# Landmark attention layer: value blocks stationary in four column tiles, both attention maps divided by their sums before the difference

## The reference, cut to what matters

```python
xn = _rms(x, w_norm_in)                      # x * rsqrt(mean(x*x) + 1.19e-07) * w
ssm_out = <running mean over the tokens, a decay for each head>
q1, q2, k1, k2 = xn @ slr_wq1, xn @ slr_wq2, xn @ slr_wk1, xn @ slr_wk2   # 32 features each
v = xn @ slr_wv                                                             # 32 features
a1 = softmax(q1 @ k1.T * sc);  a2 = softmax(q2 @ k2.T * sc)                 # 512 x 512 each
slr_out = ((a1 - slr_lam * a2) @ v) @ slr_wo
mixed = ssm_out + (p_medium + p_full) * slr_out     # p: a small router; plus a landmark term on the last token
out = concatenate([mixed, xn]) @ mix_w
out = residual + _rms(out, w_norm_out)
out = out + 0.1 * <the mean of out over the tokens, through three 128 x 128 matrices>
```

## Time and profile before

| what | us |
|---|---|
| median of 3 runs (2606.91 to 2615.31) | 2607.51 |
| the profiled execution, its own time | 2612.94 |
| its span in the trace | 2611.2 |
| the layer in question, 1269.7 to 1418.2 of the span | 148.5 |
| PE busy in the layer | 136.8 |
| DVE busy in the layer | 80.1 |
| ACT busy in the layer | 53.9 |
[...]

### The profile page before, as it was taken

How to read it: one execution, slowest core, us unless ns; L and a number is a source line. 1 busy time by engine, 2 the same in 40 slices (tenths; PEclk the granted TensorE clock), 3 DMA queues, 4 the chain that set the end, 5 groups by cost and what they waited for, 6 DMA issues and landing times. The chain is left out here.

```text
span 2611.2 us, 30132 instructions
## 1 busy us (share of the span) xinstructions
PE 2225.1 (85%) x9848; PEld 923.0 (35%) x9888; DVE 1703.9 (65%) x2464; ACT 1216.5 (47%) x2420; POOL 699.1 (27%) x658
## 2 busy tenths in 40 slices
PE   8999999947469989787998779988878988878877
PEld 2333224312122224354454234433324436533332
DVE  5666665568877745653463664569995446569995
ACT  4655663258557853221342225346655422246653
POOL 1111110042211110121100010049981013149882
PEclk9999999979889989897866889999999999999989
DMA  3000000033000010000000000022220000012220
GB/s 162 1 1 1 1 1 1 1 49 50 1 2 1 1 59 38 1 1 1 0 1 1 1 0 1 0 74 98 87 69 1 0 1 2 1 62 94 93 78 17
DMA packets 24281, 68.64 MB, mean 26 GB/s; under 512 B 2816, under 2 KB 9024, under 8 KB 23360
## 3 DMA queue, kind: packets, MB, share of 16 engines
q1 hardware_dynamic: 23264, 65.94, 8.2%
q10 hardware_dynamic: 864, 0.79, 0.3%
HBM read 58.78 MB, written 1.57 MB: 23 GB/s over the span
## 5 line engine op out<-in xcount | busy, mean ns | idle before, releaser
L3816 POOL TENSOR_TENSOR l_drive<-l_du,l_bsb 128x1024 f32<-128x1024 f32 x126 | 296.4, 2374 | 41.4 <-DVE l_du L3717 26.3
L3568 DVE TENSOR_TENSOR_SCAN l_state<-l_decay,l_drive 128x1024 f32<-128x1024 f32 x128 | 289.9, 2278 | 10.0 <-ACT l_decay L3509 9.3
L3398 PE MATMUL l_py<-l_state,w_const 128*128 128x512 f32 x512 | 256.9, 628 | 41.5 <-DVE l_state L3576 29.8
L241 POOL TENSOR_TENSOR l_nx_small<-l_nx_small,w_norm 128x4 f32<-128x4 f32 x50 | 53.4, 1068 | 866.4 <-DVE l_nx_small L234 866.4
L403 ACT ACTIVATE l_probs<-l_psp,l_stats 128x512 f32<-128x512 f32 x256 | 173.1, 683 | 147.1 <-DVE l_stats L413 147.1
L3509 ACT ACTIVATE l_decay<-l_delta,l_a 128x511 f32<-128x511 f32 x256 | 164.9, 680 | 119.8 <-DVE l_state L3568 119.6
L1324 DVE TENSOR_REDUCE l_tops<-l_ring 128x2 f32<-128x1024 f32 x128 | 151.5, 1220 | 45.6 <-PE l_ring L1315 45.2
L411 DVE TENSOR_REDUCE l_stats<-l_psp 128x2 f32<-128x1024 f32 x128 | 156.1, 1219 | 29.3 <-PE l_psp L363 28.9
L760 DVE SCALAR_TENSOR_TENSOR l_product<-l_psu,w_gated,l_first 128x512 f32<-128x512 f32 x104 | 78.0, 750 | 131.8 <-ACT l_first L734 131.5
L1396 ACT ACTIVATE l_shared<-l_ring 128x512 f32<-128x512 f32 x256 | 139.0, 598 | 46.1 <-PE l_ring L1386 45.9
L3398 PEld LDWEIGHTS l_py<-l_state,w_const 128*128 128x128 f32 x512 | 100.3, 200 | 153.8 <-issue 87.1
(11 more groups left out here) (623 smaller groups left out, 4242.5 us busy)
## 6 DMA issues: line engine op xcount, KB each, us to landing
l_bsb<-l_rows SPq DMA_DIRECT2D x64, 512.0 KB, 3.7
l_csb<-l_rows SPq DMA_DIRECT2D x32, 256.0 KB, 3.1
l_stack<-l_parts SPq DMA_DIRECT2D x84, 64.0 KB
w_gated<-in_gated SPq DMA_DIRECT2D x1, 3297.5 KB, 10.3
w_mha<-in_mha SPq DMA_DIRECT2D x1, 2568.5 KB, 11.4
w_ssm<-in_ssm SPq DMA_DIRECT2D x2, 1171.0 KB, 14.3
w_moe<-in_moe SPq DMA_DIRECT2D x1, 2248.0 KB, 18.3
w_const<-in_const SPq DMA_DIRECT2D x1, 1131.0 KB, 13.6
```

Of the source, the lines that this page charges most:

```text
L3398: mm = pe.matmul(py[:, t, :], eye, state[:, k % STATES, t, :], start=False, stop=k % NS == NS - 1, skip_group_check=True)
L3568: dve.tensor_tensor_scan(state[:, k % STATES, :, :].rearrange("p t s -> p (t s)"), decay[:, k % 2, :, :].rearrange("p t s -> p (t s)"), dr ...
L3816: pool.tensor_tensor(drive[:, k % RING, :, :], du[:, :, :], bsb[:, k // 2 % RING, k % 2, :].unsqueeze(1).to_broadcast([P, CT, S]), ALU.mult)\
```

## The change

`average` takes the value block (128 x 32) as the stationary operand and the whole turned map row block (512 columns) as the moving one: four matmuls, each into its own 32 PSUM partitions, one for each key block, in column tiles 0, 32, 64 and 96 of the array. The sum over the key blocks is left to `project_ctx`, whose weight `wo` is now stacked four times (K = 128). With the features already on partitions, `turn_ctx` and `divide_ctx` go, and the batch's chain has one step less; STEPS is 25. `differ` divides each map by its own sum before subtracting, with one more DVE instruction over 128 x 512. `var_in` and `var_out` take the form of `NextNorm.var`: the constant stationary in four column tiles, 128 columns moving, and DVE picks each row's own token with two instructions in place of one. `make_diag_out`, `nx.keep` and `nx.diag` go from DVE to ACT (`keep_by_scalar` L208, `diag_by_scalar` L251: four instructions with 128 x 128 elements each).

New steps: average 4b+6 with take_ctx in the same step, project_ctx and join_parts 4b+7, join and take_mix 4b+8, var_out, eps_out and rstd_out 4b+9, spread_out and make_diag_out 4b+10, bus and scale_out 4b+11, take_bus and finish 4b+12, centre, square and keep 4b+13, nx.var 4b+14, nx.eps, nx.rstd and nx.diag 4b+15, nx.spread and nx.scale 4b+16. On ACT a step is: exp_scores, take_bus, take_turn, take_ctx, take_mix, make_diag_out, nx.square and keep, nx.diag.

```diff
@@ var_in (var_out likewise, on sq_out and mx)
-                mm = pe.matmul(bank(b)[:, t:t + 1], sq[:, b, tok(t)], mean, start=True, stop=True, skip_group_check=True)
+                mm = pe.matmul(bank(b)[t * QUAD:(t + 1) * QUAD, 0:P], mean, sq[:, b, tok(t)], start=True, stop=True,
+                               skip_group_check=True, tile_position=(0, t * QUAD))
@@ average
-            for t in range(TT):
-                for o in range(TT):
-                    mm = pe.matmul(mx[:, b % 2, t * SH:(t + 1) * SH], turned[:, b % 2, o, tok(t)], v[:, b, o, :],
-                                   start=o == 0, stop=o == TT - 1, skip_group_check=True)
+            for o in range(TT):
+                mm = pe.matmul(mx[o * SH:(o + 1) * SH, b % 2, :], v[:, b, o, :], turned[:, b % 2, o, :], start=True, stop=True,
+                               skip_group_check=True, tile_position=(0, o * SH))
             mm.then_inc(L["averaged"].sem, 1)
-        def turn_ctx(pe, b):
-            pe.wait_ge(L["ctx"].sem, L["ctx"].at(0, b + 1))
-            for t in range(TT):
-                mm = pe.transpose(mx[0:SH, b % 2, tok(t)], ctx[:, t, :], eye)
-            mm.then_inc(L["ctx_turn"].sem, 1)
@@ spread_out
-            pe.wait_ge(L["diag_out"].sem, L["diag_out"].at(0, b + 1))
+            pe.wait_ge(L["diag_out"].sem, L["diag_out"].at(0, TT * (b + 1)))
@@ take_ctx
-            act.wait_ge(L["ctx_turn"].sem, L["ctx_turn"].at(0, b + 1))
+            act.wait_ge(L["averaged"].sem, L["averaged"].at(0, b + 1))
             act.wait_ge(L["slr"].sem, L["slr"].at(0, b))
-            act.activation(ctx_t[:, :], mx[0:SH, b % 2, :], ACT.Copy).then_inc(L["ctx_sb"].sem, 1)
+            act.activation(ctx_t[:, :], mx[:, b % 2, :], ACT.Copy).then_inc(L["ctx_sb"].sem, 1)
@@ eps_in (eps_out likewise)
-            dve.tensor_scalar(small[:, b, 0, :], bank(b)[:, 0:TT], RMS_EPS, None, ALU.add).then_inc(L["eps"].sem, 1)
+            dve.scalar_tensor_tensor(own_in[:, b, :], bank(b)[:, 0:P], RMS_EPS, own, ALU.add, ALU.mult)\
+                .then_inc(L["own"].sem, 1)
+            dve.wait_ge(L["own"].sem, L["own"].at(0, b + 1))
+            dve.tensor_reduce(small[:, b, 0, :], own_in[:, b, :].rearrange("p (j c) -> p j c", j=TT), AX.X, ALU.add)\
+                .then_inc(L["eps"].sem, 1)
@@ differ
-            dve.reciprocal(ratio[:, 0:1], second).then_inc(L["ratio"].sem, 1)
-            dve.wait_ge(L["ratio"].sem, L["ratio"].at(0, 2 * u + 1))
-            dve.scalar_tensor_tensor(out=ratio[:, 1:2], in0=first, scalar=w("slr_lam"), in1=ratio[:, 0:1], op0=ALU.mult,
-                                     op1=ALU.mult).then_inc(L["ratio"].sem, 1)
-            dve.wait_ge(L["ratio"].sem, L["ratio"].at(0, 2 * u + 2))
-            dve.scalar_tensor_tensor(out=probs[:, u % 3, 0, :], in0=probs[:, u % 3, 1, :], scalar=ratio[:, 1:2],
-                                     in1=probs[:, u % 3, 0, :], op0=ALU.mult, op1=ALU.subtract)\
+            dve.reciprocal(ratio[:, :], sums[:, b % 2, :, t]).then_inc(L["ratio"].sem, 1)
+            dve.wait_ge(L["ratio"].sem, L["ratio"].at(0, 3 * u + 1))
+            dve.tensor_scalar(ratio[:, 1:2], ratio[:, 1:2], w("slr_lam"), None, ALU.mult).then_inc(L["ratio"].sem, 1)
+            dve.wait_ge(L["ratio"].sem, L["ratio"].at(0, 3 * u + 2))
+            dve.tensor_scalar(probs[:, u % 3, 1, :], probs[:, u % 3, 1, :], ratio[:, 1:2], None, ALU.mult)\
+                .then_inc(L["ratio"].sem, 1)
+            dve.wait_ge(L["ratio"].sem, L["ratio"].at(0, 3 * u + 3))
+            dve.scalar_tensor_tensor(out=probs[:, u % 3, 0, :], in0=probs[:, u % 3, 0, :], scalar=ratio[:, 0:1],
+                                     in1=probs[:, u % 3, 1, :], op0=ALU.mult, op1=ALU.subtract)\
                 .then_inc(L["mixp"].sem, 1)
-        def divide_ctx(dve, b):
...
@@ make_diag_out
+        def make_diag_out(act, b):
+            act.wait_ge(L["rstd_out"].sem, L["rstd_out"].at(0, b + 1))
+            act.wait_ge(L["spread_out"].sem, L["spread_out"].at(0, b))
+            to, mask = diag_out[:, :, :].rearrange("p t (j c) -> p t j c", j=TT), own_tokens(core)
+            for j in range(TT):
+                act.activation(to[:, :, j, :], mask[:, :, j, :], ACT.Copy, scale=small[:, B, 1, j:j + 1])\
+                    .then_inc(L["diag_out"].sem, 1)
@@ STEPS and the order of the steps
-        STEPS = TT * (inner - 1) + 18 if inner == B else TT * (B - 1) + 14
+        STEPS = TT * (inner - 1) + 17 if inner == B else TT * (B - 1) + 13
...
@@ weights
-                "wo": v[p + "slr_wo"], "r1": v[p + "router_w1"], "r2": v[p + "router_w2"],
+                "wo": np.tile(v[p + "slr_wo"], (TT, 1)), "r1": v[p + "router_w1"], "r2": v[p + "router_w2"],
```

More of the change, by code:

```diff
@@ L2202, in landmark_layer @@
     L = Layer(nc, name, core, ["slr"], **NextNorm.SIGNALS, **NextNorm.LAST, lam=2, chain=3, chain_sb=3,
-              sq=B, var=B, eps=B, rstd=B, diag=B, spread=B, xl=B, drive=B, ema=B, wide_q=B,
+              sq=B, var=B, own=B, eps=B, rstd=B, diag=B, spread=B, xl=B, drive=B, ema=B, wide_q=B,
               q=B, q_sb=B, k=B, k_sb=B, v_ps=B, v_sb=B,
               hid=1, hid_sb=2, lscore=1, arc=8, lexp=1, wide=3, logit=1, router=7, rexp=1,
-              scores=NU, highest=NU, top=NU, probs=2 * NU, ratio=2 * NU, mixp=NU, turn=NU, turn_sb=NU,
-              averaged=B, inv=B, ctx=B, ctx_turn=B, ctx_sb=B, slr=B, joined=2 * B, mix=B, sq_out=B, mix_sb=B,
-              var_out=B, eps_out=B, rstd_out=B, diag_out=B, spread_out=B, scaled=B, result=B, bus=B, bus_sb=B,
+              scores=NU, highest=NU, top=NU, probs=2 * NU, ratio=3 * NU, mixp=NU, turn=NU, turn_sb=NU,
+              averaged=B, ctx_sb=B, slr=B, joined=2 * B, mix=B, sq_out=B, mix_sb=B,
+              var_out=B, own_out=B, eps_out=B, rstd_out=B, diag_out=TT * B, spread_out=B, scaled=B, result=B, bus=B, bus_sb=B,
               done=B)
@@ L2240, in landmark_layer @@
         front = mx[:, 1, :]
-        nx = NextNorm(L, aux[:, :])
+        nx = NextNorm(L, aux[:, :], pieces=TT)
         late = NextNorm(L, aux[:, :], last=True, shared=nx)
         eye, ones = core.w("const", "eye"), core.w("norm", "ones")
-        mean = core.w("norm", "mean", 0, 1)
+        mean, own = core.w("norm", "mean"), core.w("norm", "own")
         score_scale = 1.0 / float(SH) ** 0.5
@@ L2665, in _ @@
                     if b is not None:
-                        turn_ctx(pe, b)
+                        project_ctx(pe, b)
                     b = batch_at(u, 8)
                     if b is not None:
-                        project_ctx(pe, b)
+                        join(pe, b)
                     b = batch_at(u, 9)
                     if b is not None:
-                        join(pe, b)
-                    b = batch_at(u, 10)
-                    if b is not None:
                         var_out(pe, b)
-                    b = batch_at(u, 14, inner)
+                    b = batch_at(u, 13, inner)
                     if b is not None:
                         nx.centre(pe, b)
-                    b = batch_at(u, 17, inner)
+                    b = batch_at(u, 16, inner)
                     if b is not None:
@@ L2683, in _ @@
                         turn(pe, u - 2)
+                    b = batch_at(u, 10)
+                    if b is not None:
+                        spread_out(pe, b)
                     b = batch_at(u, 11)
                     if b is not None:
-                        spread_out(pe, b)
-                    b = batch_at(u, 12)
-                    if b is not None:
                         bus(pe, b)
-                    b = batch_at(u, 15, inner)
+                    b = batch_at(u, 14, inner)
                     if b is not None:
@@ L2782, in _ @@
                     if b is not None:
-                        make_diag_out(dve, b)
-                    b = batch_at(u, 12)
-                    if b is not None:
                         scale_out(dve, b)
                     b = batch_at(u, 15, inner)
-                    if b is not None:
-                        nx.keep(dve, b)
-                    b = batch_at(u, 16, inner)
                     if b is not None:
@@ L2807, in _ @@
                     b = batch_at(u, 16, inner)
-                    if b is not None:
-                        nx.diag(dve, b)
-                    b = batch_at(u, 17, inner)
                     if b is not None:
@@ L2840, in _ @@
                 for u in range(STEPS):
-                    b = batch_at(u, 10)
+                    b = batch_at(u, 9)
                     if b is not None:
                         rstd_out(b)
-                    b = batch_at(u, 16, inner)
+                    b = batch_at(u, 15, inner)
                     if b is not None:
```

59 lines of the change are left out of this document (26 added, 33 removed).

## The result

The changed kernel takes 2589.3 us in the median of four runs (2586.2 to 2592.4), the kernel before 2608.9 on the same chip; the ratio is 0.9924, 95% interval 0.9907 to 0.9940. The forecast was 2596.2 with a range of 2585 to 2605. So the sign and the range held, but the gain is 19.6 us and not 11.3. The profiled execution spans 2587.0 us against 2611.2; that is 24.2, more than the medians' 19.6, mainly because the profiled execution of the kernel before was itself 4.0 us above its median (2612.94 against 2608.92).

A forecast was written before the change was run, and what follows sets the result against it. PE's queue was taken to set the layer's pace, at a mostly lower clock. Terms -1.5 + 0.7 - 4.7 - 0.5 - 1.9 - 3.4 summed to -11.3 us, from median 2607.51 to 2596.2, range 2585 to 2605.

The forecast's parts named there:

- Front: Layer's start: early variances shrink from 5.12 to under 2 us, some 2.3 reaching the first spread; -1.5 us, bounds -2.3 and 0.
- Steps 0 to 6: DVE's step grows from 2.44 to about 2.9 us, still under PE's 3.05; +0.7 us, bounds 0 and +1.3.
- First period: Average(0) to average(1): 23.5 us becomes 18.8 with the shorter average and no turn_ctx; -4.7 us.
- less 1.9 because the clock rose in its last part: Average(0) to average(1): 1.9 us taken off the lower-clock sums, 25.4 before and 20.2 after.
- Second period: Average(1) to average(2): less PE work, but a new 2.2 us wait at spread_out for ACT's diagonal; -0.5 us, bounds -2 and +2.
- Third period: Average(2) to average(3): work 18.9 to 16.2 us, waits 2.8 to 3.9; -1.9 us.
- Tail: Last average to layer end, at the lower clock: 31.7 us becomes 28.3, savings partly handed back by diagonals, epsilons and a wait; -3.4 us.
- The price of a switch between array shapes: PE's switch into and out of column tiles, read off another layer's row: at most 0.15 us.
- The likeliest case: The forecast itself: the layer's six parts sum to -11.3 us, giving 2596.2, own range 2592 to 2601; chance 0.53.
- the first rival: Narrow work kept the clock down; full-width tiles let it stay at 2.4 GHz through the batches: 2588 us, chance 0.20.
- The slower side: PE has more gaps and never gets the upper clock; layer's mean clock near 0.5: 2617 us, chance 0.07.
- The two remaining rivals: Half lost to PE waits as DVE's step passes PE's: 2602.5, chance 0.17; average's tiles not side by side: 2608, chance 0.03.

The follow-up runs named there:

- the repetition: The changed kernel run once more, word for word; layer 131.0 us instead of 126.5, ratio to the kernel before 0.9927 (0.9910 to 0.9943).

## Why the prediction was right or wrong, by its own steps

1. Front: -1.5 forecast with bounds of -2.3 and 0, -3.0 in the profile and -4.2 in the repetition. The work was priced right: four variances are 2.3 us of PE instead of 6.2, and the first spread comes 2.3 us earlier on the layer's own count, as forecast. But the clock did not rise "at the same moment as now": it rose 13.1 us into the layer before and 9.4 after, so the gain was not partly spent at a clock of 0.50.
2. Steps 0 to 6: +0.7 forecast, +1.0 measured, +1.6 in the repetition. The price of 0.48 us for the multiply was 0.486, and DVE's step is 2.96 us for 2.9, still under PE's 3.05.
3. First period: -4.7 forecast, -10.2 and -7.4 in two executions. This and the tail (6) are the terms that were mis-sized: together they gave 9.0 us more than forecast in the profile, of 11.4 in all, and 7.2 more in the repetition, of 6.9 in all. The step that failed here is "less 1.9 because the clock rose in its last part", kept the same before and after. The rise came 74.5 us into the layer before (1344.4 less 1269.9), 53.7 after (1325.9 less 1272.2) and 58.6 in the repetition, so 16 to 21 us earlier. The work that I took out was priced right: 2.0 forecast, 1.94 measured.
4. Second period: -0.5 forecast, -1.0 and +3.6. The new wait was foreseen with its cause and its place. In the repetition, with the average ahead of it at a clock of 0.50, it was 2.3 us against the 2.2 of the forecast; in the profile, with the average at 1.00, it is 2.8, because ACT was still busy with the exponentials for 0.5 us when the turn was done. POOL's power was done before. In all PE sat idle 4.2 us here, not 2.2; that the term came near the forecast in the profile is luck, since PE's work at a clock of 1.00 instead of 0.81 paid for it.
5. Third period: -1.9 forecast, -2.6 and -3.9. This agreement is luck too. PE's idle time was 7.9 us where 3.9 was forecast (2.6 instead of 1.0 ahead of the join, and 1.8 ahead of var_out that was not in the sum), and its work took 11.5 us where 16.2 was forecast, at a clock of 0.91 instead of 0.69. The term doesn't follow from its own numbers either: (16.2 + 3.9) less (18.9 + 2.8) is -1.6.
6. Tail: -3.4 forecast, -6.9 and -7.9. Again the clock. The step that failed is "At the lower clock after the last average starts": it was at 0.72 and 0.78, and the average itself took 1.07 us and not 2.1. Diagonals and waits came as priced or longer, with 1.9 and 2.3 us of PE idle ahead of the last two spread_out. "Is partly handed back by two diagonals" held in direction: with both diagonals on DVE the tail is 2.4 us shorter at the same clock of 0.72.

The step "that keep and diag leave DVE is worth nothing by itself here" held in that no gain came of it. By the ratios, the variances and the moves to ACT together changed nothing that can be measured (0.9924 with them, 0.9920 without).

The price of a switch between array shapes was read off a row whose neighbours are not whole-array work but bf16 matmuls with 64 rows, so it did not show what it was used for. The traces show it elsewhere: ahead of a tiled group a whole-array matmul of 512 columns moves PE on by 0.95 us, ahead of another of its kind by 0.86 (1262.68 to 1263.63 and 1261.83 to 1262.68 in the kernel before). That is 0.1 us, so the small price stands.

The likeliest case was thus the wrong one of two that both forecast a gain. The measured 2589.3 lies outside the range of that case alone, 2592 to 2601; the whole range of 2585 to 2605 held because it made room for the first rival, that the narrow work had kept the clock down. That rival gave 2588 and had a chance of 0.20. Its mechanism held in the profile and only in part in the repetition: it gave the three periods 51 us, the forecast 56.7, and they were 49.9 and 56.1. In the repetition the periods together thus came out as the forecast had them, with other parts, and what went beyond it lay in the front and the tail. The row for that rival was there: from 1322.7 to 1329.6 PE was busy without a gap at a clock of 0.50. The slower side rested on the opposite reading, that gaps cost the clock, which no run shows; PE's busy share fell from 92% to 77% of the layer and the clock rose from 0.66 to 0.80, while in the kernel before a PE that the profile calls busy for 29.7 us on end stayed at 0.50. The two remaining rivals fall. The tiles run side by side (1.94 us, not 6.8). The waits are there, PE's idle time in the layer grew from 12.4 to 29.5 us, but PE's busy time fell by more, and DVE's multiply took 0.486 us and not the 0.75 that this rival needed.

What stays open: which of the properties of the narrow matmuls matters, the 32 columns, or the weight load in front of each (32 loads of 128 columns in each average, now 8 of 32). Both went together in every run. It was not tried apart. Nor was it tried what the scores (32 rows) and the turns do to the clock, which stayed at 0.50 under them, nor why the rise comes earlier in one execution of the same kernel than in another.

## What to carry to other kernels

Price a change of TensorE work twice, at the clock of before and at the clock that the new mix of work will be granted (here 0.66 and 0.80 in the layer): a block of matmuls with few moving columns can cost more than its own time, here some 25 us for 14.4 us of work when it was put back. If the profile has PE at 100% and the granted clock at 0.5, as in the kernel before from 1322.7 to 1329.6, look for such a block, and try turning its operands round so that the long side moves. Take a second execution of the same kernel before reading a difference of a few us out of one profile. And before a small instruction is given to another engine, look at what stands in front of it in that engine's queue: of the 9.8 us that PE waited for the diagonal, 2.8 went when it was put ahead of the 0.95 us of copies on ACT, and 8.5 when it went back to DVE.

## What the runs showed of the hardware that was not expected

- A PE that the profile shows as busy without a gap can stay at the lower clock for long: 29.7 us in the kernel before (1314.6 to 1344.3), 16.4 us in the changed kernel's repetition, at a granted clock of 0.50.
- Wide matmuls added to a layer whose PE was 92% busy cost nothing that could be measured: 1.0002 (0.9983 to 1.0020) with sixteen more, since the layer's granted clock went from 0.66 to 0.78.
- The same program's layer differed by 4.5 us between two executions (126.5 and 131.0), with the clock's rise at 53.7 and 58.6 us into the layer; the spans differed by 5.9 us (2587.0 and 2592.9).
- Four 32-column tiles of float32 by 512 columns take 1.94 us at a granted clock of 0.50 and 1.07 at 1.00, where one whole-array matmul takes 2.08 and 1.13: here a group of four tiles cost no more than one matmul.
